# An attention and feed-forward kernel's upper SBUF region, moved down by 64 bytes

## What is computed

```python
mod = silu(c) @ ada_w.T + ada_b                      # six vectors per batch item, two gates through tanh
h = modulate(rmsnorm(x, g1, D), scale_msa, shift_msa)
q, k, v = split(h @ qkv_w.T + qkv_b)                 # rmsnorm of q and k per head, q * 36 ** -0.5
attn = softmax(einsum('bhqd,bhkd->bhqk', q, k))
o = einsum('bhqk,bhkd->bhqd', attn, v) @ proj_w.T + proj_b
x = x + gate_msa * o
h2 = modulate(rmsnorm(x, g2, D), scale_mlp, shift_mlp)
x = x + gate_mlp * (gelu(h2 @ fc1_w.T + fc1_b) @ fc2_w.T + fc2_b)
```

## Time and profile before

| what | us |
|---|---|
| median of 3 runs (2937.09 to 2938.67) | 2937.92 |
| the profiled execution's own time | 2937.97 |
| its span, first to last instruction | 2936.2 |
| phase one, about | 463 |
| attention, about | 1422 |
| rest of the projection, feed-forward | 1051 |

### The profile page before, as it was taken

How to read it: one execution, slowest core, us unless ns; L and a number is a source line. 1 busy time by engine, 2 the same in 40 slices (tenths; PEclk the granted TensorE clock), 3 DMA queues, 4 the chain that set the end, 5 groups by cost and what they waited for, 6 DMA issues and landing times.

```text
span 2936.2 us, 35353 instructions
## 1 busy us (share of the span) xinstructions
PE 2891.7 (98%) x13030; PEld 2183.2 (74%) x13030; DVE 1980.2 (67%) x2702; ACT 1578.8 (54%) x1921; POOL 208.6 (7%) x150
## 2 busy tenths in 40 slices
PE   7999997999999999999999999999999999999999
PEld 7999995666666666666666666788888888888887
DVE  6777767998988888888888887844343242424342
ACT  3433325767767767767767766634344343434342
POOL 1232310011000000000000000080000000000000
PEclk9999998999999999999999999999999999999999
DMA  6465554223223222223222223442222222322121
GB/s 225 138 202 169 175 172 133 76 60 86 77 73 88 76 62 84 77 73 87 77 64 81 76 74 97 125 133 87 73 85 73 81 78 80 102 89 85 41 68 50
DMA packets 238454, 282.67 MB, mean 96 GB/s; under 512 B 34960, under 2 KB 144016, under 8 KB 237392
## 3 DMA queue, kind: packets, MB, share of 16 engines
q1 hardware_dynamic: 233696, 271.33, 30.3%
q10 hardware_dynamic: 4592, 9.18, 0.9%
HBM read 195.50 MB, written 84.67 MB: 95 GB/s over the span
## 4 chain that ended last, share of the span: by engine, by line
PE 82%; DVE 1%; ACT 1%; issue 0%; ACTq 0%; DVEq 0%
PE ps L1500 16%; PE ps L1525 16%; PE ps L1585 15%; PE ps L1567 15%; PE ps L1512 14%; PE ps L1543 4%; PE ps L1511 2%; ACT gated L1207 1%; DVE x L1382 0%; DVE w_lo L1375 0%; DVE x L1385 0%; DVE x L1387 0%; ACT p_r L1151 0%; DVE tmp L1384 0%; PE ps L1555 0%
## 5 line engine op out<-in xcount | busy, mean ns | idle before, releaser
L1151 ACT ACTIVATE p_r<-ps 128x1024 f32<-128x1024 f32 x512 | 491.7, 1024 | 412.1 <-PE ps L1500 412.0
L1330 DVE TENSOR_TENSOR p_lo<-p_r,p_hi 128x1024 fp32r<-128x1024 f32 x512 | 612.8, 1217 | 0.0
L1500 PE MATMUL ps<-qT,kT 110*128 110x512 f32 x2048 | 573.2, 397 | 6.3 <-issue 6.0
L1500 PEld LDWEIGHTS ps<-qT,kT 110*128 110x128 f32 x2048 | 382.4, 189 | 140.5 <-issue 58.4
L1151 ACT ACTIVATE prob<-ps 128x1024 f32<-128x1024 f32 x512 | 483.4, 1030 | 1.0 <-PE ps L1500 0.5
L1511 PE MATMUL ps<-prob,vp 128*64 128x512 f32 x1024 | 453.1, 595 | 0.0
L1453 DVE TENSOR_TENSOR a_lo<-act,a_hi 128x512 fp32r<-128x512 f32 x144 | 102.7, 713 | 517.5 <-ACT a_hi L1194 517.5
L1512 PE MATMUL ps<-prob,vp 128*37 128x512 f32 x1024 | 451.7, 594 | 0.0
L1324 DVE CAST p_hi<-p_r 128x1024 fp32r<-128x1024 f32 x512 | 349.9, 693 | 135.0 <-ACT p_r L1151 133.6
L1585 PE MATMUL ps<-a_hi,w 128*128 128x512 f32 x1296 | 415.5, 393 | 0.6 <-DVE a_lo L1453 0.6
L1525 PE MATMUL ps<-p_hi,vx 128*128 128x512 f32 x1024 | 404.3, 395 | 0.1
(11 more groups left out here) (170 smaller groups left out, 3586.4 us busy)
## 6 DMA issues: line engine op xcount, KB each, us to landing
w_raw<-w SPq DMA_DIRECT2D x144, 320.0 KB, 2.9
qk_hi_scratch<-aw SPq DMA_DIRECT2D x32, 576.0 KB, 3.2
qk_lo_scratch<-aw SPq DMA_DIRECT2D x32, 576.0 KB, 4.4
kT<-qk_hi_scratch SPq DMA_DIRECT2D x128, 144.0 KB
qT<-qk_hi_scratch SPq DMA_DIRECT2D x128, 144.0 KB
v_scratch<-stv SPq DMA_DIRECT2D x32, 512.0 KB, 2.7
vp<-v_scratch SPq DMA_DIRECT2D x16, 1024.0 KB, 9.6
xb<-xT SPq DMA_DIRECT2D x8, 1280.0 KB, 10.7
```

Of the source, the lines that this page charges most:

```text
L1151: act.activation(out, ps[:, 2 * slot:2 * slot + 2, :].rearrange("p a b -> p (a b)"), ACT.Exp).then_inc(exp_done, 1)
L1330: dve.tensor_tensor(p_lo[:, j], p_r[:, j], f32(p_hi[:, q % HIGHS]), ALU.subtract).then_inc(plo_done, 1)
L1500: mm = pe.matmul(ps[:, 2 * (entry % RING) + h, :], kT[r][:, h, kt * P:(kt + 1) * P], qT[:, u % 2, h], start=True, stop=True)
```

## The change

`W2` is rounded down to a multiple of 128. It becomes 146304 instead of 146368, and everything in the upper region is 64 bytes lower and starts at a multiple of 128. `OB` becomes 102272, which is still above the end of the lower region. No instruction is added, taken away or reordered, no wait and no size is changed. Offsets within the upper region, one tensor against another, are as before; those between the two regions shrink by 64.

```diff
     top = nc.sbuf_top // 64 * 64
     low_end = (nc.sbuf_base + 63) // 64 * 64
-    W2 = top - 8 * FC * D
+    W2 = (top - 8 * FC * D) // 128 * 128
     WP = W2 - 4 * 2 * KC * DP
     OB = WP - 4 * (KC + KF) * BLK
```

## The result

The changed kernel takes 2952.85 us (median of 5 runs, 2951.47 to 2953.65) against 2937.92: slower by 0.51%, the ratio 1.0051 with an interval of 1.004 to 1.0063. The forecast was no change: 2937.9 us, in a range of 2934.8 to 2941.0.

What follows compares the result with a forecast made beforehand. TensorE, busy for 98% of the span, was taken as the bound; every term (matmuls, VectorE, ScalarE, GpSimd, DMAs) was 0, so the forecast stayed at 2937.9 us, range 2934.8 to 2941.0, rivals left out.

Steps and rivals of the forecast that it cites:

- The bound: Whole kernel: TensorE is busy for 98% of the span, so phase two costs what its matmuls cost.
- the matmul part: Split values, fc2 and projection: 4624 matmuls that read the upper region change by 0 ns, 2.3 us to either side.
- The cleanest pair is the projection against fc1: Matmuls of the same form, operands off a multiple of 128 against at one: medians 389 and 389 ns.
- I take 0 ns for each: Each of the 4624 matmuls reading the upper region was taken to cost nothing more or less after the move.
- no matter of the offset: fc2: 392 ns over a_hi and 388 over a_lo, both aligned with weights of the same w2, so not the offset.
- What lifts the median is in the attention loop, not in the address: Split values: medians of 394 and 393 ns, 4.5 above the projection's 389, were put down to the attention loop.
- VectorE, ScalarE, GpSimd, the DMAs: Other engines and transfers on the upper region: 0 each, with idle time or lead covering any small change.
- The slower rival: Attention scores, L1500: regions in step make score matmuls meet ScalarE's and VectorE's traffic; +9.2 us, 2947.1 us; chance 0.04.
- The faster rival: Attention, L1525: split values lose their 4.5 ns, 9.2 us, so 2928.7 us; chance 0.07.
- both rivals: The two SBUF collision cases in attention: split values faster, chance 0.07, and scores slower, chance 0.04; 9.2 us each way.
- the row with 4.5 ns: Split values' medians of 394 and 393 ns against the projection's 389; it left the collision cases a price.

Runs made afterwards that it cites:

- e5: Against the kernel before: the whole upper region 192 bytes lower, at equal offsets with the lower region; 2935.9 us.
- e13: Against the kernel before: upper region 192 bytes lower, and scores read 128 rows instead of 110, the added rows holding constants; 2916.4 us.
- e8: Against the kernel before: osb, rlb and lt 64 bytes higher in attention, everything from w1_hi on 64 higher in the feed-forward; 2954.8 us.
- e1: Against the kernel before: upper region 128 bytes lower, so again 64 past a multiple of 128; 2953.3 us.
- e6: Against the kernel before: attention's upper buffers 512 bytes higher, act32, a_hi and a_lo 192 higher, w2 not moved; 2937.3 us.

## Why the prediction was wrong, point by point

**The bound** was right, and it's why so little could cost so much: TensorE has no slack, and the 14.5 us of the two stages are 2.4 ns a matmul over 6112 of them (scores, split values, fc2).

**The step that failed** is in the matmul part: "The cleanest pair is the projection against fc1", and "I take 0 ns for each". It asked whether a buffer off the multiple is slow. Both lines of the pair keep weights and moving operand in one region, so in both the offset between the operands is 0. They measure the one thing that the change leaves alone. The lines that the change touches are those that take an operand from each region, which is fc2, and those that take turns with matmuls on the other region, which are the scores and the split values. fc1 and the projection were no comparison for these, and after the change they do stand at 389 as forecast.

**The row that knew better** was fc2's: 392 ns for `a_hi` against fc1's 389, with an aligned moving operand and weights from the other region. The prediction named it and put it down as "no matter of the offset", since `a_lo` against the same `w2` has 388. But fc2's steps from start to start repeat at 226, 229 and 232 ns (medians by place), and one row of three can well hold the cheap one. On average the slice was dear: 3.21 against 3.17 us once the offsets were equal (e5).

**"What lifts the median is in the attention loop, not in the address"** was half right. The 226.9 ns of the 16 last split values come from their not being mixed with scores. The lift comes from the mixing, and how much it lifts depends on the offsets and the rows: e13 removes it.

**VectorE, ScalarE, GpSimd, the DMAs** were right at 0: 1218 to 1220, 686 to 687 and 1025 to 1027 ns, which their idle time covers, and no new wait.

**The slower rival**, "the regions fall into step", had the sign and one of the places, L1500 with 395 ns. Its mechanism was wrong. It blamed ScalarE's and VectorE's traffic, which has no part in fc2's loss (the comparison behind e8) nor, for the output buffers, in attention (e8). And regions wholly in step, e13, are the fastest of all, once the rows are equal too. The price, +9.2 us for the scores alone, was near attention's +8.8 by luck; the 5.7 us of fc2 were nowhere in the case. **The faster rival** fell: L1525 went up.

**The range** was too narrow because its width was the resolution of a comparison, +-2.3 us, rather than the doubt whether it was the right comparison. The spread of 389 to 394 between lines of one form was an effect without an explanation. It holds 2048 x 4.5 + 2048 x 3 + 1296 x 3 ns, 19 us in all, and the change moved the addresses under it.

**The rule on contention.** The prediction lowered the chance of both rivals for the rule in the Trainium skill, SBUF — State Buffer, section "SBUF: two separate sides", that TensorE never waits on anyone. As for other engines, no run contradicts it: e8 moved output buffers with no effect, and fc2's steps are the same beside a busy VectorE and an idle one. What it leaves no room for is a cost among TensorE's own operands, and there is one here; whether that is a wait in SBUF isn't shown. The rule lowered the rivals' chances and put no number on the row with 4.5 ns. The Trainium skill, TensorE: Matmul & The Clock Gate, section "Back-to-back issue gap", gives the step by the number of columns alone, for 512 some 216 ns by its formula for a single gap and some 131 ns for a sustained stream. Here steps of the same 512 columns average 226.6 to over 233 ns by placement (e5's fc2 with 3.17 us for 14, e1's with 3.27), so the measurement decides: neither figure fits, and neither knows of the placement.

The chain of e1 in the feed-forward, for the last number:

```profile
2306.75 3.27 PE ps L1585 x14
2310.02 3.20 PE ps L1567 x14
2313.22 3.27 PE ps L1585 x14
```

## What to carry to other kernels

Where TensorE is the bound, compare the medians of matmuls of one form across lines, and the time of equal slices in the chain, since a median hides a few slow steps. If they aren't all equal, try the operands of neighbouring matmuls at equal offsets modulo 256 bytes together with equal numbers of rows: in attention both together gained 14.0 us, the offsets alone lost 4.7 and the rows alone gained 1.6. A "rounder" alignment of one region alone can lose. A comparison inside the trace bounds a change only if the thing that the change alters differs between its two sides; here it was the relation between two buffers, and the pair compared had the same relation twice. A spread between rows of one form that has no explanation belongs in the range.

## What the runs showed of the hardware that was not expected

- The step of a float32r matmul of 128x512 depends on where its operands lie: fc2's slice of 14 takes 3.17 us with equal offsets, 3.21 at 192, 3.25 at 128 and 3.27 at 64.
- The period is 256 bytes in attention: its upper buffers at +64, -192 and +320 give +4.7, +4.7 and +4.9 us, at 0 and +512 give 0 and -0.4.
- A border between matmuls that don't match disturbs the matmuls behind it by a fixed sequence of steps between 224 and 236 ns, which runs out to 227 ns after at most ten in fc1's slices (e6, e1 and the kernel before).
- A change between 110 and 128 rows from one matmul to the next costs time of its own kind: at equal offsets, attention takes 1417.0 us with equal rows and 1435.7 without, so that reading 18 rows of constants more is 18.7 us faster.
